# Cross-attention with scores and exponentials in halves of one PSUM bank, maxima over four banks, the value bias on POOL, and casts moved in the self-attention

## The reference

```python
# 1: cross-attention, 16 heads of 32, 4096 keys
q = qdq(ln(x)) @ qdq(wq).T + bq ; k, v = split(ctx @ wkv.T + bkv)
o = softmax(q k^T / sqrt(32)) v ; x = x + qdq(o) @ qdq(wp).T + bp
# 2: causal self-attention, 4 groups of 4 query heads of 128, 256 keys
x = x + attn(ln(x), weight_qkv) @ weight_proj.T
# 3: feed-forward, 2048 wide
x = x + (silu(g) * u) @ w_down.T
```

## Time and profile before

| | |
|---|---|
| median of 3 runs | 606.46 us (604.95 to 606.72) |
| the profiled execution's own time | 607.84 us |
| its span | 605.8 us |
| granted TensorE clock, mean | 0.993 |
| PE, PEld, DVE, ACT, POOL busy | 97%, 78%, 64%, 50%, 37% |
| heads: from the first score of head 1 to that of head 15 | 14.1 us a head |

### The profile page before, as it was taken

The page is one execution under the profiler, slowest core; times in us unless marked ns, Lnnn a source line. Parts: engine busy times, 40 slices in busy tenths (PEclk is TensorE's granted clock), DMA queues, the critical chain, the costliest instruction groups (busy, mean ns, idle before and its releaser), DMA issues.

```text
span 605.8 us, 12502 instructions
## 1 busy us (share of the span) xinstructions
PE 590.1 (97%) x4270; PEld 470.5 (78%) x4270; DVE 387.4 (64%) x704; ACT 301.4 (50%) x439; POOL 225.0 (37%) x110
## 2 busy tenths in 40 slices
PE   8999999999999999999999999999997999999997
PEld 7888888888887666766676676766897889799996
DVE  4999330330334889999999888997664234376662
ACT  3545233233232666655666655565358477654441
POOL 0000100000002788878888888870103445400000
PEclk9999999999999999999999999999999899999999
DMA  8965734624639655655545555500140334256410
GB/s 290 328 224 191 226 109 157 208 78 156 214 101 285 187 159 156 188 161 159 170 152 152 156 171 159 156 34 1 56 154 1 139 100 179 70 198 206 163 60 36
DMA packets 34223, 92.20 MB, mean 152 GB/s; under 512 B 6928, under 2 KB 11024, under 8 KB 30480
## 3 DMA queue, kind: packets, MB, share of 16 engines
q1 hardware_dynamic: 32944, 89.68, 45.6%
q10 hardware_dynamic: 1248, 2.10, 0.9%
HBM read 65.02 MB, written 18.35 MB: 138 GB/s over the span
## 4 chain that ended last, share of the span: by engine, by line
PE 88%; ACT 5%; DVE 3%; issue 1%; DMA 1%; POOL 0%; ACTq 0%; POOLq 0%; SPq 0%; DVEq 0%
PE ps L346 16%; PE ps L347 16%; PE ps L348 16%; PE ps L1567 10%; PE ps L1555 9%; PE ps L1429 9%; PE ps L1581 3%; ACT p_ring L768 3%; PE ps L1533 1%; ACT h_ring L854 1%; DVE m_part L1052 1%; PE ps L1638 1%; DMA f_ring<-stream 1%; PE ps L1447 1%; PE ps L1521 1%
## 5 line engine op out<-in xcount | busy, mean ns | idle before, releaser
L1052 DVE TENSOR_REDUCE m_part<-ps 128x1 f32<-128x512 f32 x240 | 150.6, 681 | 17.8 <-PE ps L1429 17.6
L768 ACT ACTIVATE p_ring<-ps 128x1024 f32<-128x1024 f32 x128 | 124.5, 1022 | 69.0 <-PE ps L1567 28.3
L617 POOL TENSOR_TENSOR p_sum<-p_sum,p_ring 128x1024 f32<-128x1024 f32 x42 | 100.1, 2384 | 3.7
L1555 PEld LDWEIGHTS ps<-q_stack,k_stack 98*128 98x128 f32 x512 | 74.9, 189 | 16.3 <-ACT p_ring L768 6.5
L1555 PE MATMUL ps<-q_stack,k_stack 98*128 98x256 f32 x512 | 85.2, 289 | 1.2
L1429 PE MATMUL ps<-k_stack,q_max 96*128 96x512 f32 x240 | 85.4, 416 | 0.1
L1567 PE MATMUL ps<-p_ring,v_head 128*32 128x256 f32 x960 | 64.6, 383 | 0.0
L1011 DVE SCALAR_TENSOR_TENSOR kl_buf<-ps,biases,kh_buf 128x512 fp32r<-128x512 f32 x32 | 23.7, 748 | 58.8 <-ACT kh_buf L718 58.6
L319 DVE TENSOR_TENSOR l_ring<-f_ring,h_ring 128x2048 fp32r<-128x2048 f32 x22 | 50.2, 2287 | 12.5 <-ACT h_ring L315 12.5
L1429 PEld LDWEIGHTS ps<-k_stack,q_max 96*128 96x128 f32 x240 | 41.1, 188 | 20.2 <-DVE m_part L1052 12.8
L346 PE MATMUL ps<-xt_h,h_ring 128*128 128x256 f32 x200 | 56.0, 280 | 0.0
(11 more groups left out here) (224 smaller groups left out, 1175.7 us busy)
## 6 DMA issues: line engine op xcount, KB each, us to landing
f_ring<-stream SPq DMA_DIRECT2D x29, 1024.0 KB, 5.0
k_stack<-kh_scratch SPq DMA_DIRECT2D x128, 128.0 KB, 2.6
kh_scratch<-kh_buf SPq DMA_DIRECT2D x32, 256.0 KB, 5.5
kl_scratch<-kl_buf SPq DMA_DIRECT2D x32, 256.0 KB, 5.6
k_stack<-kl_scratch SPq DMA_DIRECT2D x64, 128.0 KB, 2.7
v_head<-v_all SPq DMA_DIRECT2D x16, 512.0 KB, 3.0
v_all<-stream SPq DMA_DIRECT2D x4, 256.0 KB, 4.8
f_ring<-stream SPq DMA_DIRECT2D x4, 256.0 KB, 5.6
```

The costliest lines, as they stand in the source:

```text
L617: nc.gpsimd.tensor_tensor(p_sum[:, p, :], p_ring[:, 0, :] if n == 0 else p_sum[:, p, :], p_pair[:] if c == 3 else p_ring[:, c % 4, :], ALU ...
L768: nc.scalar.activation(p_ring[:, c % 4, :], ps[:, 2 * (c % 2):2 * (c % 2) + 2, :].rearrange("p b n -> p (b n)"), ACT.Exp, scale=XSCALE).th ...
L1052: nc.vector.reduce_max(m_part[:, j // NT, j % NT:j % NT + 1], maximum_bank(j), AX.X).then_inc(max_read, 1)
L1555: last = nc.tensor.matmul(ps[:, 2 * (c % 2) + k // 2, (k % 2) * N:(k % 2 + 1) * N], k_stack[p][0:SPLIT_ROWS + MAX_ROWS, at128(4 * c + k)], ...
```

## The change

It has five parts.

1. Scores and exponentials come in halves: 2 matmuls into one bank, then one exponential of 512 columns. The halves use banks 0, 1, 2 in turn, so half n (0 to 15 in a head) waits for the exponential of half n - 3. The wait for a free slot of `p_ring` stands before the first half of a chunk.
2. The maximum tiles use four banks (4, 3, 6, 5), and a tile waits for the read of the tile four before it. `maximum_rows` no longer waits for the next head's tile 0 to be read. One tile of head 1 instead of two is made ahead of it.
3. In PE's order, score 5 goes behind values 0 to 3, and tile 13 before them: score 4, tiles 12, 13, values 0 to 3, score 5, tiles 14, 15, tile 0 of the next head but one.
4. The value bias is added by POOL to `v_all` in the context stage (32 additions of 128 x 512), and no longer by DVE to the output; the two DVE instructions there become one. SP's first loads of values wait for POOL's last addition.
5. In the self-attention the first group's `half_high(0, .)` moves ahead, one half before the first exponentials and one behind the first query; in all groups `half_high(1, .)` moves one place back, its halves behind the exponentials of tiles 0 and 1 of the next group.

`minus_magic` is also made 32 columns wide instead of 16.

```diff
@@ maximum and score banks
         def maximum_bank(j):
-            return bank((5, 4, 6)[j] if j < 3 else 4 + j % 3)
+            return bank((4, 3, 6, 5)[j % 4])
+        def score_bank(half):
+            return bank(half % 3)
@@ SP
-            sp.wait_ge(v_evac, MT)
+            sp.wait_ge(v_biased, MT)
             for h in range(2):
                 load_v(h, h)
@@ POOL
             nc.gpsimd.memset(k_stack[0][SPLIT_ROWS:P, :].bitcast(F32), 1.0).then_inc(ones_set, 1)
+            def add_value_bias(c):
+                for mt in range(4):
+                    pool.wait_ge(v_evac, 4 * c + mt + 1)
+                    at = v_all[:, :, 4 * c + mt, :]
+                    nc.gpsimd.tensor_tensor(at, at, bv_row[:].rearrange("p (h d) -> p h d", d=DH),
+                                            ALU.add).then_inc(v_biased, 1)
+            pool.wait_ge(rows_loaded, 32)
+            pool.wait_ge(ones_set, 2)
+            with pool.Fori(0, NCTX - 1) as c:
+                add_value_bias(c)
             pool.wait_ge(k_done, KT * NCTX)
...
             nc.gpsimd.memset(k_stack[1][SPLIT_ROWS:P, :].bitcast(F32), 1.0).then_inc(ones_set, 1)
+            pool.wait_ge(ones_set, 3)
+            add_value_bias(NCTX - 1)
@@ ACT exponentials(h)
-                    act.wait_ge(s_done, 8 * h + c + 1)
-                    wait(act, pv_done, 8 * h + c - 3)
...
-                    nc.scalar.activation(p_ring[:, c % 4, :], ps[:, 2 * (c % 2):2 * (c % 2) + 2, :].rearrange(
-                        "p b n -> p (b n)"), ACT.Exp, scale=XSCALE).then_inc(exp_done, 1)
+                    for half in range(2):
+                        act.wait_ge(s_done, 16 * h + 2 * c + half + 1)
+                        if half == 0:
+                            p_ring_free(h, c, last)
+                        nc.scalar.activation(p_ring[:, c % 4, half * 2 * N:(half + 1) * 2 * N], score_bank(2 * c + half),
+                                             ACT.Exp, scale=XSCALE).then_inc(exp_done, 1)
@@ ACT group(g) of the self-attention
                 if first:
                     next_query(0)
+                    half_high(g, 0, 1)
...
-                if first:
-                    half_high(0, 0)
                 exponential(3, g)
...
-                if first:
-                    half_high(0, 1)
                 if more:
                     next_query(1)
-                    half_high(1, 0)
...
                     exponential(0, g + 1)
-                    half_high(1, 1)
+                    half_high(g, 1, 0)
                     normalize(0, g + 1)
                 output_high(3)
                 if more:
                     exponential(1, g + 1)
+                    half_high(g, 1, 1)
                     normalize(1, g + 1)
...
+            half_high(0, 0, 0)
             for j in range(2):
                 exponential(j, 0)
@@ DVE normalize_output(h), and the same in normalize_last_output
-                for t in range(NT):
-                    nc.vector.scalar_tensor_tensor(out=o_all[:, t, bass.ts(h, DH)], in0=added[:, t, :],
-                                                   scalar=r_den[:, t:t + 1], in1=bv_row[:, bass.ts(h, DH)],
-                                                   op0=ALU.mult, op1=ALU.add).then_inc(o_done, 1)
+                nc.vector.tensor_tensor(o_all[:, :, bass.ts(h, DH)], added, r_den[:].unsqueeze(2).to_broadcast([P, NT, DH]),
+                                        ALU.mult).then_inc(o_done, NT)
@@ PE maxima
+                    early = isinstance(h, int) and h < 3
+                    if isinstance(h, int) and h == 1 and j < 2:
+                        pe.wait_ge(max_read, 16)
+                        if j == 1:
+                            pe.wait_ge(v_evac, MT)
                     elif j == 2:
                         wait(pe, o_done, NT * (h - 2))
+                        if early:
+                            pe.wait_ge(max_read, 16 * h - 1)
-                    elif j == 4:
+                    elif j == 3:
                         pe.wait_ge(mrow_ready, h)
                     else:
-                        pe.wait_ge(max_read, 16 * h + (j - 1 if j == 3 else j - 2))
+                        pe.wait_ge(max_read, 16 * h + j - 3)
@@ PE maximum_rows
-                if not (isinstance(h, int) and h == H - 1):
-                    pe.wait_ge(max_read, 16 * h + 17)
@@ PE scores
-                wait(pe, exp_done, 8 * h + c - 1)
-                for k in range(4):
...
+                for half in range(2):
+                    n = 2 * c + half
+                    wait(pe, exp_done, 16 * h + n - 2 if n > 2 else 16 * h + (0, -2, -1)[n])
+                    for k in range(2):
...
+                    last.then_inc(s_done, 1)
@@ PE head
                 score(4)
-                next_maxima(12, 13)
-                score(5)
-                next_maxima(13, 15)
+                next_maxima(12, 14)
                 for c in range(4):
                     value(c)
-                next_maxima(15, 16)
+                score(5)
+                next_maxima(14, 16)
```

More of the change, by code:

```diff
@@ L758, in exponentials, with p_ring_free @@
                         evacuate_output(h - 1)
-                    act.wait_ge(s_done, 8 * h + c + 1)
-                    wait(act, pv_done, 8 * h + c - 3)
[L761 to L767, removed]
-                    nc.scalar.activation(p_ring[:, c % 4, :], ps[:, 2 * (c % 2):2 * (c % 2) + 2, :].rearrange(
-                        "p b n -> p (b n)"), ACT.Exp, scale=XSCALE).then_inc(exp_done, 1)
+                    for half in range(2):
[4 more added lines that the diff above has]
+                                             ACT.Exp, scale=XSCALE).then_inc(exp_done, 1)
+            def p_ring_free(h, c, last):
+                wait(act, pv_done, 8 * h + c - 3)
+                summed = SUMS_BEFORE[c]
+                if last and c in (1, 2):
+                    act.wait_ge(pair_done, h + 1)
+                elif summed is not None:
+                    wait(act, sums_done, NSUMS * h + summed)
+                elif c >= 6:
+                    act.wait_ge(pair_done, h + 2 if last else h + 1)
             maximum_row(0, 0)
@@ L834, in normalize, with half_high @@
                                          scale=s_inv[:, j % 2, st:st + 1]).then_inc(pn_ready, 1)
+            def half_high(g, w, half):
+                if half == 0:
+                    act.wait_ge(f_loaded[w], 16 * (g + SQ0 // 2 + w))
+                at = slice(half * KT // 2, (half + 1) * KT // 2)
+                ins = nc.scalar.copy(h_ring[w][:, at, :], f_ring[w][:, at, :])
+                if half == 1:
+                    ins.then_inc(h_ready, 1)
             def group(g):
@@ L847, in output_high @@
                     nc.scalar.copy(ot_h[:, j, :], bank(3)[:, 0:N]).then_inc(oth_ready, 1)
[L849 to L856, removed]
                 def next_query(u):
@@ L868, in group @@
                 if more and not first:
-                    half_high(0, 0)
+                    half_high(g, 0, 0)
                 normalize(2, g)
                 if more and not first:
-                    half_high(0, 1)
+                    half_high(g, 0, 1)
                     next_query(0)
@@ L1158, in add_last @@
             def add_last(n, chunk):
-                dve.wait_ge(exp_done, 8 * (H - 1) + chunk + 1)
+                dve.wait_ge(exp_done, 16 * (H - 1) + 2 * chunk + 2)
                 dve.wait_ge(sums_done, NSUMS * (H - 1) + n)
@@ L1552, in scores @@
                     pe.wait_ge(v_evac, MT)
-                wait(pe, exp_done, 8 * h + c - 1)
-                for k in range(4):
-                    last = nc.tensor.matmul(ps[:, 2 * (c % 2) + k // 2, (k % 2) * N:(k % 2 + 1) * N],
-                                            k_stack[p][0:SPLIT_ROWS + MAX_ROWS, at128(4 * c + k)],
-                                            q_stack[p][0:SPLIT_ROWS + MAX_ROWS, :], start=True, stop=True)
-                last.then_inc(s_done, 1)
+                for half in range(2):
+                    n = 2 * c + half
+                    wait(pe, exp_done, 16 * h + n - 2 if n > 2 else 16 * h + (0, -2, -1)[n])
+                    for k in range(2):
+                        last = nc.tensor.matmul(score_bank(n)[:, k * N:(k + 1) * N],
+                                                k_stack[p][0:SPLIT_ROWS + MAX_ROWS, at128(4 * c + 2 * half + k)],
+                                                q_stack[p][0:SPLIT_ROWS + MAX_ROWS, :], start=True, stop=True)
+                    last.then_inc(s_done, 1)
             def values(h, p, loads, c):
-                pe.wait_ge(exp_done, 8 * h + c + 1)
+                pe.wait_ge(exp_done, 16 * h + 2 * c + 2)
                 if c == 0:
```

29 lines of the change are left out of this document (12 added, 17 removed).

## The result

| | before | after |
|---|---|---|
| median of 4 runs each | 605.9 us (604.95 to 606.72) | 618.03 us (617.51 to 618.12) |
| the profiled execution's own time | 607.84 us | 618.07 us |
| its span | 605.8 us | 616.3 us |
| granted TensorE clock, mean | 0.993 | 1.000 |

The ratio is 1.0199, with a 95% interval of 1.0185 to 1.0213: slower by 12.1 us, beyond the forecast's 609.0 and beyond its range to 611.8. The sign was the forecast's, the size was not.

A forecast was written before the change was run, and what follows sets the result against it. PE's chain bounds a head (14.1 us); after the change, loops through POOL set 14.5. Heads +5.8, last head and tail -0.4, casts -2.8 sum to +2.6 on 606.46: 609.0 us, 8-in-10 range 602.0 to 611.8.

The forecast's parts named there:

- Loop B: Heads: loop over one head, from S through PE's tiles, DVE's pair and POOL's four sums to S again: 14.53 us.
- S: Second half of score 3 (half 7) on PE, in the bank E4 frees; forecast 0.73 us after POOL's last sum.
- Loop A: Heads: loop over two heads through PE, DVE's ten tiles, the pair and POOL's sums: 28.98 us, 14.49 a head.
- Four maximum banks: Start of the heads: tiles run further ahead, 1.1 us won in head 0, already 0.6 lost in head 1.
- E4: ACT's exponential of chunk 2's first half in a head; waits for POOL's last sum of the head before, taken as 0.59 us.
- Casts: Self-attention: earlier first-group casts -3.6 us, late query cast in the next group +0.8, sum -2.8, bounds -5 and -0.5.
- a difference that I leave out: The profiled execution's 607.84 us stands 1.4 above the median of the runs, 606.46; the forecast gave this no term.
- The faster heads: Rival 1: the wait before score 2 goes and S finds E4 done; 13.8 us a head, total 597.7; chance 0.12.
- the heads as before: Rival 2: the wait at S only replaces that at score 2; heads 0 to -1, total about 602.7; chance 0.20.
- Rival 4: Context stage to head 0: the value bias holds head 0, +1.3 and what queues behind it, 610.3; chance 0.03.
- Rival 3: Self-attention: PE's waits still bring the 0.51 clock, casts gain only 0.5, total 611.4; chance 0.15.
- E0: ACT's exponential of the first half of score 0 in a head; forecast to start with half a score.

The follow-up runs named there:

- x3: The kernel before with only `minus_magic` widened from 16 to 32 columns: 608.84 us, ratio 1.0043.
- x4: The changed kernel with `minus_magic` put back from 32 to 16 columns: 615.67 us, ratio 1.0155.
- x5: The kernel before with part 5 alone, the moved casts of the self-attention: 604.49 us, ratio 0.9982.
- x10: The kernel before with `minus_magic` 48 columns wide instead of 16, casts as before: 605.72 us, ratio 1.0014.
- x7: The kernel before with part 4 alone, value bias added by POOL and one DVE instruction at each output: 605.22 us, ratio 1.0.
- x1: The changed kernel with DVE adding the pair before maximum tiles 10 and 11 instead of behind them: 611.58 us, ratio 1.0086.
- x11: The changed kernel with parts 4 and 5 and the width of `minus_magic` put back, leaving parts 1 to 3: 617.78 us, ratio 1.0206.

## Why the prediction was right or wrong

**Heads: the loop was right, one term of it was too small.** Loop B is the chain that came. Its terms, as forecast and as measured in the changed kernel:

| term | forecast | measured |
|---|---|---|
| POOL's last sum to S | 0.73 | 0.73 (347.55 to 348.28) |
| S and refill | 0.50 | 0.51 |
| tile 9, denominators | 0.81 | 0.80 |
| from PE's tile 10 to the pair | 1.34 (0.66 for the tiles, 0.68 for the read) | 1.67 (349.59 to 351.26) |
| pair to POOL's sum | 1.38 | 1.38 |
| four sums | 9.77 | 9.75 |

The step that failed is "then DVE reads tile 11 (0.68)". I let DVE start where PE ends tile 11, as if it had read tile 10 by then. But in the forecast's own 0.66 for the two tiles, tile 10 is there after 0.44 and tile 11 comes 0.22 behind it, while DVE reads one in 0.64: DVE stands waiting for tile 10, since the denominators lie between tiles 9 and 10 on PE (0.30 idle, above), and reads both behind it, one after the other. That is 0.33, and it takes the head from 14.53 to 14.86; 14.88 was measured. Loop A, at 14.49, has no say then; the idle 0.30 before tile 10 shows that DVE is not held by its own work. A small term, but every head pays it, and the heads' own loss went from +0.4 to +0.8.

**How many heads pay.** I counted 13 periods and +0.6 for the start. The first period alone grew from 13.66 us (202.87 to 216.53) to 14.97 (203.74 to 218.71), where before it was shorter than a steady head; and the last two heads paid as well (+1.2; the last period of pairs is 14.78 us where it was 14.00). Heads and tail came to +11.4 where the forecast had +5.4. Of the 6.0 between them, 3.9 are the 12 periods from the second pair to the fourteenth (+9.1), 0.5 the start (+1.1 at the second pair, counted from the last value copy, where +0.6 was forecast) and 1.6 the end (+1.2, where -0.4 was).

**Four maximum banks.** The forecast put the first pair at 201.2 against 201.7. Counted from the last value copy it came 0.2 earlier, not 0.5, and as predicted nothing of it is left in head 1.

**E4.** 0.599 measured, 0.59 taken from the copy of the same shape. The Trainium skill (ScalarE: Activation LUTs, What ACT_TABLE_LOAD costs) gives 186 ns and 0.833 ns an element for an activation with immediate scale and bias, an estimated 0.61 us here. The trace agrees: 0.599.

**`minus_magic`.** The forecast has no term for it. The text reported "made 32 columns wide" and priced it at nothing without saying so. It costs 2.4 to 2.6 us by the medians of x3 and x4, and 2.0 by their profiled executions: 0.6 to 0.7 in the context stage, 1.15 in the feed-forward, 0.2 or less in the self-attention. This is the second largest part of the miss.

**Casts.** The move of the casts was forecast well: in x5 PE goes on at 474.86, 44.0 us behind the last `x_hat` of the second norm, where the forecast's 474.7 is 44.3 behind it; the second wait came too, and against the profiled execution the stage is 3.2 us shorter (-2.8 forecast). What failed is "a difference that I leave out": the profiled execution stood above the median because the low clock was in it, and the casts' gain was largely that low clock (x10, at 1.00 with the casts of before, has 99.76 us for the stage, x5 99.63). A gain that is read from the profiled execution can't be taken off a median that doesn't contain the loss. Against the median the part is worth 0.9 us.

**Value bias and tail.** The bias cost nothing, as forecast; the last addition came at 195.28, behind the last tile, and held nobody (x7). The 0.4 forecast for the last head and the output did not come: the shorter output brought nothing (x7), and the last heads lost.

```profile
195.28 1.28 POOL L611 TENSOR_TENSOR v_all<-v_all,bv_row 128x512 f32<-128x512 f32 x1 [1.97 <-ACT v_all L749]
```

**The miss in one line.** 618.0 - 609.0 = 9.0: 6.0 from the heads, 2.2 from the context stage and the feed-forward (1.7 to 1.9 of it `minus_magic` by x3 and x4, the rest not told from the spread), 1.4 from the difference left out, less some 0.6 of small terms (the casts' 0.4, and 0.3 between own time and span).

**Rivals.** The faster heads and the heads as before needed POOL or the wait at S to be less late than the rows said; they weren't, and x1 shows that even without the loop three banks don't reach 14.1. Rival 4 (the value bias holds head 0) fell with x7. Rival 3 (the clock falls all the same) fell: the window of the changed kernel that answers to the low one, 480.5 to 487.5, is at 1.00.

```profile
480.50:487.50 7.00, 6.09 (x34) 4.90 (x33) 1.85 (x6) 5.08 (x15) 4.59 (x1) 1.00 0.00 0
```

**What stays open.** That 14.45 in x1 is the wait for E0 and nothing else was read from its trace and not tried by taking that wait away. The heads alone (x11, at a mean clock of 1.000 616.09 against 605.05) give +11.0, the traces +11.4. That the place of the tensors behind `minus_magic` makes the products slower is what is left when the width is ruled out, not shown, and which tensor it is wasn't tried either. Why the clock fell in one execution and not in another with the same waits stays open.

## What to carry to other kernels

When a ring of buffers is made shorter, ask which release each slot now waits for, and follow that releaser back through all engines to where it waits for the same ring: if it closes, add it up, with every instruction of an in-order queue that starts only when its producer is there, not only the last one. A profiled execution that stands above the median holds something the others don't; find it before a gain is read out of it. An edit that looks like padding has a price until it is measured.

## What the runs showed of the hardware

- **With the tensors moved by 64 bytes a partition, products of 256 columns were slower.** With `minus_magic` 64 bytes wider, the float32r products of the feed-forward went from 279 ns to 284, 283 and 281; with 128 bytes to 281 (x10); the run's time grew by 2.4 to 2.6 us (x3, x4) and by 0.4. The trace has no addresses: that the place of the tensors declared behind it is the cause is my reading of these runs.
- **The same waits of PE came with a low clock in one execution and not in another.** The kernel before had PE at 0.51 for seven microseconds in its profiled execution, behind two waits that sum to 2.2 us, and x10, with the same order of casts and the same two waits (1.24 and 0.99), had 1.00 there in its own. By the two levels, PE ran at 1.2 GHz in the one and at 2.4 in the other. Without these waits no execution of 35 had a mean clock below 0.999.
- **POOL beside a busy ACT and PE.** 32 additions of 512 columns in place took 1.34 us each on the average, more than the 1.2 that half of a 1024 column sum gives, and cost the run nothing (x7, ratio 0.999 to 1.001).
- **A short activation.** An exponential of 512 columns from PSUM took 0.599 us on the average (256 of them), one of 1024 columns 1.022.
